# Attention with a quantised side branch on one core: three products per score stack, one wide evacuation, layer norm on ScalarE, fewer regrouping DMAs

## The reference

```python
xn = layernorm(x)                                   # x: (16, 512, 256), fp32
qkv = xn @ w_qkv.T + b_qkv                          # 16 heads of 16
att = q @ k.T / 4 + hope_bias                       # bias: sum of cos/sin of (i - j)
att = softmax(where(causal, att, -inf))
attn = (att @ v) @ w_proj.T + b_proj
ffn = bf16(fp8(bf16(xn) / s_in) @ fp8(kernel / s_k) * (s_in * s_k)) + bias
out = x + attn + ffn
```

## Time and profile before

| | us |
|---|---|
| median of 3 runs | 1071.23 |
| lowest, highest | 1069.98, 1076.69 |
| span of the profiled execution, first to last instruction | 1065.8 |

### The profile page before, as it was taken

How to read it: one execution, slowest core, us unless ns; L and a number is a source line. 1 busy time by engine, 2 the same in 40 slices (tenths; PEclk the granted TensorE clock), 3 DMA queues, 4 the chain that set the end, 5 groups by cost and what they waited for, 6 DMA issues and landing times.

```text
span 1065.8 us, 22454 instructions
## 1 busy us (share of the span) xinstructions
PE 946.5 (89%) x6608; PEld 611.8 (57%) x6608; DVE 798.5 (75%) x1417; ACT 556.0 (52%) x1033; POOL 463.2 (43%) x434
## 2 busy tenths in 40 slices
PE   4588989989898999989999898989989899999992
PEld 3355556656565665656556565656656566665652
DVE  7686877878787787868778787877878787786721
ACT  3125565554546555455655545465554556555560
POOL 4133534525363452536345253634525363452541
PEclk9578999989999998989999899998989899898996
DMA  7644536365563636556363655636365463536421
GB/s 175 112 98 86 111 54 113 89 119 116 95 130 63 128 72 123 113 100 124 64 127 74 120 114 97 127 63 127 74 116 120 93 129 65 114 68 122 95 59 46
DMA packets 81750, 107.47 MB, mean 101 GB/s; under 512 B 19264, under 2 KB 39360, under 8 KB 81728
## 3 DMA queue, kind: packets, MB, share of 16 engines
q1 hardware_dynamic: 81296, 106.69, 50.5%
q10 hardware_dynamic: 432, 0.52, 0.2%
HBM read 18.81 MB, written 8.91 MB: 26 GB/s over the span
## 4 chain that ended last, share of the span: by engine, by line
PE 52%; DVE 20%; SPq 9%; DMA 9%; issue 7%; ACT 2%; DVEq 1%; POOL 0%; ACTq 0%; POOLq 0%
PE pv L551 10%; SPq L285 8%; PE scoreT_b L539 7%; PE scoreT_a L539 6%; DVE xn L755 5%; DMA stacks<-qk_parts 5%; PE misc_a L454 5%; PE score_b L523 5%; PE misc_b L454 5%; DVE neg_max L781 4%; PE score_c L523 4%; PE score_a L523 4%; DVE qk_parts L774 3%; DMA xn<-recips 2%; DVE neg_max_parts L789 2%
## 5 line engine op out<-in xcount | busy, mean ns | idle before, releaser
L991 POOL TENSOR_SCALAR_AFFINE_SELECT probs<-probs 128x512 f32<-128x512 f32 x256 | 163.3, 643 | 406.0 <-ACT probs L701 405.4
L701 ACT ACTIVATE probs<-scoreT_b 128x512 f32<-128x512 f32 (+1 forms) x352 | 196.3, 558 | 178.6 <-PE scoreT_b L539 175.4
L701 ACT ACTIVATE probs<-scoreT_a 128x512 f32<-128x512 f32 (+1 forms) x352 | 196.6, 558 | 153.3 <-PE scoreT_a L539 148.6
L781 DVE TENSOR_REDUCE neg_max<-score_a 128x1 f32<-128x512 f32 (+3 forms) x240 | 153.5, 639 | 83.4 <-PE score_a L525 83.2
L551 PE MATMUL pv<-probs,v_ones 128*32 128x512 f32 (+3 forms) x2048 | 196.8, 458 | 1.8 <-POOL probs L991 1.8
L539 PE MATMUL scoreT_b<-stacks 114*128 114x384 f32 (+3 forms) x512 | 174.4, 392 | 12.4 <-ACT probs L701 12.4
L781 DVE TENSOR_REDUCE neg_max<-score_b 128x1 f32<-128x384 f32 (+3 forms) x240 | 150.0, 625 | 39.8 <-PE score_b L525 34.4
L539 PE MATMUL scoreT_a<-stacks 114*128 114x128 f32 (+3 forms) x512 | 173.0, 389 | 3.1 <-ACT probs L701 2.9
L781 DVE TENSOR_REDUCE neg_max<-score_c 128x1 f32<-128x512 f32 (+3 forms) x224 | 142.3, 635 | 35.1 <-PE score_c L525 34.5
L523 PE MATMUL score_a<-stacks 112*128 112x512 f32 (+3 forms) x336 | 114.7, 375 | 43.4 <-DMA stacks<-qk_parts 42.8
L539 PEld LDWEIGHTS scoreT_b<-stacks 114*128 114x128 f32 x512 | 90.7, 200 | 78.1 <-ACT probs L701 47.6
(11 more groups left out here) (155 smaller groups left out, 1700.4 us busy)
## 6 DMA issues: line engine op xcount, KB each, us to landing
stacks<-qk_parts SPq DMA_DIRECT2D x512, 128.0 KB, 3.8
x_ring<-in_L_attn_x SPq DMA_DIRECT2D x16, 512.0 KB, 3.7
attn<-out_T SPq DMA_DIRECT2D x256, 32.0 KB, 1.9
xn<-recips SPq DMA_DIRECT2D x32, 256.0 KB
out<-x_ring SPq DMA_DIRECT2D x16, 512.0 KB, 3.0
stacks<-probs SPq DMA_DIRECT2D x16, 96.0 KB, 3.2
stacks<-neg_max_T SPq DMA_DIRECT2D x64, 16.0 KB
denominators<-out_T SPq DMA_DIRECT2D x64, 8.0 KB
```

Source lines behind the costliest of these rows:

```text
L701: A(PJ[j][:, h0:h0 + nh, :], STB[(SLOTS * g + k) % 2][:, 0:nh * WJ[j]] .rearrange("p (h n) -> p h n", h=nh), ACT.Exp).then_inc(exp_done, 1)
L781: V.tensor_reduce(MX[:, g % 2, h0:h0 + nh, qt], SB_[n % 3][:, 0:nh * P * (qt + 1)].rearrange("p (h w) -> p h w", h=nh), AX_X, ALU.max, neg ...
L991: GP.affine_select(out=d, in_=d, compare_op=ALU.is_ge, fill=0.0, base=0, pattern=[[0, HU], [1, P]], channel_multiplier=-1).then_inc(mask_d ...
```

## The change

It has five parts.

1. The product of low part with low part is dropped. A stack holds three products of 16 rows (`PRODS = 3`), so `K_SCORE` is 96 and `K_ALL` 98, and a stack DMA moves 48 rows. The high part stands twice in `QKP`; ACT writes both places with one instruction whose input is repeated. `QK_copy_hi` and `QK_copy_lo` are gone, and SP waits for `ql_ready`.
2. The maxima are transposed unsplit: PE transposes the 16 columns of `MX`, ACT writes the high part out of PSUM (`max_hi`), DVE the rest (`max_T`), each to partitions of its own, and SP sends them with two DMAs of one stack row each. `max_parts` is gone.
3. `normalise` moves from DVE to ACT, at the same slot (3,9), as x * rstd + (-mean * rstd). DVE computes the negated mean, POOL the product. The addition of epsilon becomes a tensor_tensor with a constant tile.
4. `v_ones` interleaves v and ones, so that results stand in even rows and denominators in odd ones. `regroup` is then one DMA of 64 partitions and one for the denominators.
5. In the start-up, one more large memset runs on POOL, and ACT normalises batch 0 ahead of its weight evacuations and batch 1 behind the first maxima.

```diff
-K_SCORE = 112
-K_ALL = 114
+PRODS = 3
+K_QK = PRODS * HD
+K_SCORE = 2 * K_QK
+K_ALL = K_SCORE + 2
...
+Q_HI, K_HI = slice(0, 2), slice(0, 3, 2)
+Q_LO, K_LO = 2, 1
...
-        QKP = sb("qk_parts", [P, 2, 4, 2, T], F32R)
-        VA = sb("v_ones", [P, TT, H, 2, HD], F32)
+        QKP = sb("qk_parts", [P, 2, PRODS, 2, T], F32R)
+        VA = sb("v_ones", [P, TT, H, HD, 2], F32)
...
-                        sp.dma_start(STK[0:64, g, a, h, :].bitcast(F32),
+                        sp.dma_start(STK[0:K_QK, g, a, h, :].bitcast(F32),
                                      QKP[r:r + HD, g // 2, :, a, :].bitcast(F32)).then_inc(stack_loaded[g], 16)
...
-                sp.dma_start(STK[K_SCORE:K_ALL, g, 0, :, :].rearrange("p h n -> p (h n)").bitcast(F32),
-                             MTS[:, g % 2, :].bitcast(F32)).then_inc(max_loaded[g], 16)
+                for part in range(2):
+                    sp.dma_start(STK[K_SCORE + part:K_SCORE + part + 1, g, 0, :, :].rearrange("o h n -> o (h n)").bitcast(F32),
+                                 MTS[:, g % 2, part, :].bitcast(F32)).then_inc(max_loaded[g], 16)
...
-                for i in range(HU):
-                    r = 64 * (g % 2) + HD * i
-                    sp.dma_start(attn_row(b)[r:r + HD, g // 2, :],
-                                 OT[32 * i:32 * i + HD, g % 2, :]).then_inc(ot_stored[g % 2], 16)
-                sp.dma_start(DEN[32 * g:32 * g + 32, :], OT[HD:P:32, g % 2, :]).then_inc(den_loaded[g % 2], 16)
+                r = 64 * (g % 2)
+                sp.dma_start(attn_row(b)[r:r + HU * HD, g // 2, :], OT[0:P:2, g % 2, :]).then_inc(ot_stored[g % 2], 16)
+                sp.dma_start(DEN[32 * g:32 * g + 32, :], OT[1:P:2 * HD, g % 2, :]).then_inc(den_loaded[g % 2], 16)
...
                     wait_alone(sp, (w_loaded, 16), (st_ready, ROW * b + SLOTS),
-                               (qh_copied, 4 * (b + 1) + 2), (ql_copied, 4 * (b + 1) + 2))
+                               (ql_ready, 4 * (b + 1) + 2))
...
-                A(qk_part(m, 0, 0), misc_of("QK", m)[:, :], ACT.Identity, bias=BQ[:, bias:bias + 1]).then_inc(qh_ready, 1)
+                A(qk_part(m, 0), misc_of("QK", m)[:, :].unsqueeze(1).broadcast_to([P, 2, T]), ACT.Identity, bias=BQ[:, bias:bias + 1]).then_inc(qh_ready, 1)
+
+            def max_hi(b, g):
+                act.wait_ge(mt_ready, 4 * b + g + 1)
+                A(MTS[:, g % 2, 0, :], misc_of("MT", (g - 1) % G)[0:HU * TT, 0:P], ACT.Copy).then_inc(mh_done, 1)
+
+            def normalise(b):
+                act.wait_ge(t_ready, 2 * b)
+                act.wait_ge(qm_done, b)
+                wait_alone(act, (w_loaded, 16), (nmr_done, b + 1))
+                for t in range(TT):
+                    ins = A(XN[:, t, :], x_slot(b)[:, t, :], ACT.Identity, scale=RSTD[:, t:t + 1],
+                            bias=NMR[:, t:t + 1])
+                ins.then_inc(xn_ready, 1)
...
-                V.tensor_scalar(VE[:, :], MV[:, :, 1], EPS, None, ALU.add).then_inc(ve_done, 1)
+                V.tensor_tensor(VE[:, :], MV[:, :, 1], EPSC[:, :], ALU.add).then_inc(ve_done, 1)
+                V.tensor_tensor(NM[:, :], MV[:, :, 0], NEG[:, :], ALU.mult).then_inc(nm_done, 1)
...
+            def max_T(b, g):
                 dve.wait_ge(mh_done, 4 * b + g + 1)
+                V.tensor_tensor(MTS[:, g % 2, 1, :], misc_of("MT", (g - 1) % G)[0:HU * TT, 0:P],
+                                MTS[:, g % 2, 0, :].bitcast(F32), ALU.subtract).then_inc(mts_ready, 1)
...
-                V.tensor_tensor(VA[:, 2 * i:2 * i + 2, :, 0, :],
+                V.tensor_tensor(VA[:, 2 * i:2 * i + 2, :, :, 0],
...
                 GP.tensor_tensor(RSTD[:, :], VE[:, :], NH[:, :], ALU.pow).then_inc(rstd_done, 1)
+                pool.wait_ge(nm_done, b + 1)
+                pool.wait_ge(rstd_done, b + 1)
+                GP.tensor_tensor(NMR[:, :], NM[:, :], RSTD[:, :], ALU.mult).then_inc(nmr_done, 1)
```

More of the change, by code:

```diff
@@ L244, in build, with qk_part @@
         out_stored = sem("out_stored")
-        def qk_part(m, part, copy):
-            pair = 2 * part + copy if m % 2 == 0 else part + 2 * copy
-            return QKP[:, m // 2, pair, m % 2, :]
+        def qk_part(m, part):
+            at = ((Q_HI, Q_LO), (K_HI, K_LO))[m % 2][part]
+            return QKP[:, m // 2, at, m % 2, :]
         def misc_of(kind, i):
@@ L651, in QK_evac @@
                 bias = [0, 2, 1, 3][m]
-                A(qk_part(m, 0, 0), misc_of("QK", m)[:, :], ACT.Identity, bias=BQ[:, bias:bias + 1]).then_inc(qh_ready, 1)
-            def QK_copy_lo(b, m):
-                act.wait_ge(ql_ready, 4 * b + m + 1)
-                A(qk_part(m, 1, 1), qk_part(m, 1, 0).bitcast(F32), ACT.Copy).then_inc(ql_copied, 1)
+                A(qk_part(m, 0), misc_of("QK", m)[:, :].unsqueeze(1).broadcast_to([P, 2, T]), ACT.Identity, bias=BQ[:, bias:bias + 1]).then_inc(qh_ready, 1)
[10 more added lines that the diff above has]
+                ins.then_inc(xn_ready, 1)
+            act.wait_ge(nmr_done, 1)
+            for t in range(TT):
+                ins = A(XN[:, t, :], x_slot(0)[:, t, :], ACT.Identity, scale=RSTD[:, t:t + 1], bias=NMR[:, t:t + 1])
+            ins.then_inc(xn_ready, 1)
             for n in range(4):
@@ L692, in attn_hi, with body @@
                 A(AH[:, ct, :], attn_row(b)[:, ct, :], ACT.Copy).then_inc(ah_ready, 1)
-            def body(b, first, last):
+            def body(b, first, last, more):
                 for g in range(G):
@@ L713, in body @@
                                 QK_evac(b + 1, i, False)
-                            for i in due(QK_AT, g, k, ACT_LAG["copy_lo"]):
-                                QK_copy_lo(b + 1, i)
+                        for i in due(MT_AT, g, k, ACT_LAG["MT"]):
+                            if not (last and i == 3):
+                                max_hi(*((b, i + 1) if i < 3 else (b + 1, 0)))
+                        if (g, k) == NORM_AT and more:
+                            normalise(b + 2)
                         if not first:
@@ L854, in _ @@
                     .then_inc(feat_parts, 1)
-            dve.wait_ge(rstd_done, 1)
-            for t in range(TT):
-                ins = V.tensor_scalar(XN[:, t, :], x_slot(0)[:, t, :], MV[:, t, 0:1], RSTD[:, t:t + 1],
-                                      ALU.subtract, ALU.mult)
-            ins.then_inc(xn_ready, 1)
             dve.wait_ge(small_loaded, 16 * 8)
@@ L942, in body @@
                             quant_magic(b + 1)
-                        if (g, k) == NORM_AT and more:
-                            normalise(b + 2)
-                    if ahead:
-                        max_parts(nb, ng)
             body(0, True, False, True)
```

108 lines of the change are left out of this document (44 added, 64 removed).

## The result

The changed kernel takes 1045.67 us (median of 5 runs, 1027.06 to 1047.74) against 1071.23: the ratio is 0.9633, with a 95% interval of 0.954 to 0.9726. That is faster, but 46.7 us above the forecast of 999 and outside its range. Three of the five runs are left out of the ratio, since their clock was lower (0.921) and their time more than 1.5% above the fastest; the median has them in, and the ratio alone would make it some 1032 us. The profiled execution took 1039.35 us with a span of 1037.6: 28.2 us less than the span before.

The account below looks back on a forecast made before the run. PE, busy 89% of the span, was taken as the bound, its waits and lower clock as winnable. Fourteen passes gain 60 us, first pass 8, start-up 3, tail 1.5: 1071.2 - 72.5 = 999 us; 8-in-10 range 980 to 1028.

Parts of the forecast that it names:

- The stack wait: PE's wait for the stack copies before g=2, 2.25 us in the pass read; it was to go entirely.
- rival A: Epsilon addition in g=2 becomes nearly free (0.17 instead of 1.20 us): 985 to 991 us, chance 0.2.
- The clean pass of 58.0: Full-clock pass of the batch loop: 61.29 less 2.25 at the stack copies and 1.0 at the pass start.
- B: Stack copies stay as dear despite fewer rows, leaving 1.3 us idle: 1019 to 1033 us, chance 0.18.
- C: ACT becomes the next in-order queue; normalisations and wide evacuation delay exponentials, 1 us in 15 passes: 1014 us, chance 0.11.
- D: Slower: an exponential on ACT waits behind the normalisations, which would eat all gains: 1082 us, chance 0.03.
- rival E: PE's idle time moves to another equal wait (reciprocals, or stack 1 at g=3), clock still falls: 1065 us, chance 0.03.
- the ruler: The one inner pass before the change with granted clock 1.00, 61.29 us long, from which the gains were reckoned.
- The reciprocals: SP's transfer that the divide in g=2 needs: 2.5 us earlier, landing near 536.3, divide at 536.65.
- Pass start: Normalisations (3.57 us) and split of the maxima (1.63) leave DVE; PE's weight load there gains about 1.0 us a pass.
- Outside the passes: Gains beyond the fourteen inner passes: first pass 8 us, start-up 3, tail 1.5.
- Around the span: The 5.4 us between the shown span of 1065.8 and the median of 1071.2 were to stay.

Follow-up runs that it names:

- the last experiment: The changed kernel with SP holding the eight copies of stack 1 back until the reciprocals have landed: 1033.56 us, ratio 0.9634.

## Why the prediction was wrong

**What held.** The stack wait is gone; the eight issues take 5.07 us (forecast 5.1). The wide evacuation takes 1.11 us (1.14), the normalisation on ACT 0.587 (0.55). The epsilon addition stayed at 1.20 us beside POOL's attn_lo (it ended at 405.54, attn_lo at 405.51), and the neighbour of the same form takes 0.15: so rival A was rightly turned down, and the rule named beside it (the Trainium skill, SBUF — State Buffer, "SBUF: two separate sides") agrees with this trace. The clean pass of 58.0 measured 58.23, but that is in part luck. In the pass from 384.90, 58.48 us long, the way to PE's start of g=2 gave 2.4 us (forecast 2.25) and the rest behind g=2 gave 1.3 (forecast 1.0), while g=2 lost 0.9 where it was to stay even: the errors cancel. Rivals B, C and D didn't occur. The mechanism of rival E did, in six passes of fourteen, and it names the wait: the reciprocals; its time, 1065 us, didn't. (The chances of the forecast and of all rivals sum to 0.98, those said to be faster to 0.92 and not 0.94; nothing hangs on it.)

**The step that failed** is "The longest idle time left is the 0.77 behind ACT, which cost the ruler no clock; so the clock should stay up and all fourteen passes come to that". Two things are wrong with it. First, it overlooked the waits inside g=2. The forecast kept the stage at 11.5 us, from its start in the ruler pass to its last wait; of these PE is busy 9.84:

```profile
533.30:544.81 11.51, 9.84 (x73) 5.80 (x73) 8.79 (x20) 7.41 (x15) 3.54 (x4) 1.00 0.66 144
541.06 0.61 PE L497 MATMUL misc_a<-ffn_w_q,xq 128*128 128x256 bf16 x4 [0.66 <-DVE neg_max_T L795]
542.10 0.51 PE L539 MATMUL scoreT_a<-stacks 114*128 114x256 f32 x2 [0.43 <-ACT probs L701]
544.81 0.33 PE L523 MATMUL score_b<-stacks 112*128 112x128 f32 x1 [0.58 <-DVE neg_max L781]
```

Three waits of 0.66, 0.43 and 0.58 us stood in the trace of before, and a stage that stays as long keeps them; after the change they are 1.60, 0.43 and 0.66 in the pass shown, and the first is 0.71 to 2.09 us in the twelve passes that have it, nearly always more than the 0.77 called the longest. The prediction read the stage's length off its ends and never asked what PE did in between. Second, it drew from one pass that the clock is safe. Such waits were survived in seven passes and not in six others. With the first pass, which fell behind the masks, that is 3.7 us in each of seven (61.91 against 58.23): 26 us of the 31 by which the fourteen passes missed.

**The reciprocals** were issued in time but took 7.25 us to the start of the divide in the pass shown (5.7 to 8.0 over the loop), where the sum had 5.7: 536.65 less the issue at 530.9. (Its "reciprocals near 536.3" would be 5.4; the two don't quite agree.) The 5.71 of the ruler pass was the shortest of the kernel before, which had 6.3 to 6.6 in the others where DVE waited for them; the copies of stack 1 right behind them slow them down, as the last experiment shows. The divide began 6.67 us behind PE's start, 1.1 later than forecast, and g=2 took 12.44 us.

**Cost of the clock.** The prediction priced a fall at 1.0 us, rightly for the kernel before. With the reciprocals earlier a fall costs 4.9 us (56.4 against 61.3): it lasts longer, and nothing else holds the stage meanwhile. I used the price of before for a kernel in which its cover was taken away, although the rival E that it belongs to says "within 1%"; its real price was higher and its chance of 0.03 far too low.

**Pass start**, forecast 1.0 us: the normalisations carry at most 0.25, the split nothing, each undone alone. Of the 1.63 us that the forecast took for the split, some 1.5 were a wait beside POOL. In the clean pass the gain was there only as part of the whole; which part held PE before isn't settled.

**Outside the passes**, forecast 12.5 us, measured -0.7. The start-up wait went from 8.86 to 6.7 us and the 4.78 of the earlier trace rows is gone, but PE has two others ahead of the first mark: 3.1 us for ACT at 63.38, and 5.0 instead of 2.8 for the low part of the transposed input. Behind the last mark the FFN wait of the last batch but one is 2.3 us long and followed by a fall as long as any, 17 us:

```profile
944.00:962.00 18.00, 17.71 (x84) 11.72 (x83) 8.00 (x14) 7.95 (x16) 9.56 (x7) 0.53 0.33 61
```

**Around the span** the 5.4 us were no constant: the profiled run of the kernel after took 1.75 us more than its span. The 5.4 were the distance of one execution's span to another execution's time.

## What to carry to other kernels

Before a wait is removed, list every idle time of the busiest engine in the stage behind it, not just the longest, and ask what covers a slow clock there once the wait is gone: the same product dropped made this kernel 1.6% slower alone and, with the reciprocals early, 5.0% faster (1067.05 to 1013.99). Two moves of a few instructions, the reciprocals' store ahead of the stack copies and the epsilon addition off DVE, then took the changed kernel from 1045.67 to 970.59 us, because they left PE no wait in g=2. A piece of unread work in a wait is a quick test of whether the clock is what is being paid.

## What the runs showed of the hardware

- Idle times of PE of 0.3 to 2.3 us, in a stage where it is otherwise busy, were followed by stretches at the lower clock (0.50) of 3.4 to 17 us in some passes and by none in others. The runs show the link, since falls vanish with the waits, but not the rule by which one pass falls and its twin doesn't.
- 256 KB twice, read from DRAM with rows repeated, could be used by DVE 5.3 to 5.7 us after the first issue with no copies behind them (7 passes), and 5.7 to 8.0 us after it beside eight copies of 96 KB.
- A DVE cast of 128x16 took 0.17 us, and 1.63 us where an instruction of POOL was running (128x1024, bf16, two inputs); in fourteen passes it ended within 0.05 us of POOL's.
- DVE's store of v at stride 2 takes 0.69 us for 512 elements; the dense one of before took 0.68.
